# A linear attention stage with its tiles turned: tokens on partitions for x, z, B and y, features on partitions for C and the logits

## The reference, cut to what matters

```python
proj = x @ W_in.T                      # xp 512, z 512, B 256, C 256, dt_low 16
dt = softplus(dt_low @ dt_W.T + dt_b)
dAcs = cumsum(dt * A, axis=2)          # within a chunk
scores = einsum('bcihn,bcjhn->bcijh', Cc, Bc) * Lm * dtc[:, :, None, :, :]
y_intra = einsum('bcijh,bcjhp->bcihp', scores, xc)
chunk_state = einsum('bckhn,bckhp->bchnp', Bc, wx)
y_cross = einsum('bcthn,bchnp,bcth->bcthp', Cc, h_states, exp(dAcs))
y = y_intra + y_cross + xp * D_param
y = y / sqrt(mean(y * y) + 1e-6) * norm_w * silu(z)
return y @ W_out.T
```

## Time and profile before

| what | value |
|---|---|
| median of 3 runs | 3202.09 us (3197.8 to 3204.78) |
| profiled execution, own time | 3200.55 us |
| its span, first to last instruction | 3198.5 us |
| PE busy | 3052.5 us, 95% |
| DVE busy | 2336.9 us, 73% |
| ACT busy | 1671.4 us, 52% |
| POOL busy | 1176.2 us, 37% |
| chain that ended last | PE 91%, DVE 5% |
| largest line in it | PE L769, 48% |

### The profile page before, as it was taken

The page is one execution under the profiler, slowest core; times in us unless marked ns, Lnnn a source line. Parts: engine busy times, 40 slices in busy tenths (PEclk is TensorE's granted clock), DMA queues, the critical chain, the costliest instruction groups (busy, mean ns, idle before and its releaser), DMA issues.

```text
span 3198.5 us, 121249 instructions
## 1 busy us (share of the span) xinstructions
PE 3052.5 (95%) x52488; PEld 2729.7 (85%) x52488; DVE 2336.9 (73%) x4256; ACT 1671.4 (52%) x3803; POOL 1176.2 (37%) x2287
## 2 busy tenths in 40 slices
PE   7999999999999999999999999998777777999999
PEld 6999999999999999999999999997666666888887
DVE  6887887887887887887887887887444445777775
ACT  5555555555555555555555555554333332555555
POOL 3554554554554554554554554553000001000000
PEclk9999999999999999999999999999999997999999
DMA  3211111111111111111111111112544344768765
GB/s 116 73 52 52 46 50 53 47 53 50 46 54 50 46 54 50 46 54 50 46 54 50 47 53 50 48 46 81 200 115 119 106 129 130 224 212 236 222 207 159
DMA packets 336353, 285.87 MB, mean 89 GB/s; under 512 B 52160, under 2 KB 265792, under 8 KB 334928
## 3 DMA queue, kind: packets, MB, share of 16 engines
q1 hardware_dynamic: 335248, 277.95, 29.3%
q10 hardware_dynamic: 576, 0.17, 0.0%
HBM read 164.80 MB, written 113.25 MB: 87 GB/s over the span
## 4 chain that ended last, share of the span: by engine, by line
PE 91%; DVE 5%; issue 3%; DMA 1%; ACT 0%; SPq 0%; POOL 0%; DVEq 0%; POOLq 0%; ACTq 0%
PE a_bank L769 48%; PE s_rt L1422 8%; PE g_pick_ps L1182 5%; PE s_w_ps L1408 5%; PE a_bank L828 4%; PE s_sum L1435 4%; PE a_bank L861 4%; DVE g_picked L1151 3%; PE g_acc_ps L1203 2%; PE a_bank L777 2%; PE a_bank L846 2%; PE a_bank L796 2%; PE a_bank L786 1%; PE a_bank L788 1%; PE a_bank L928 1%
## 5 line engine op out<-in xcount | busy, mean ns | idle before, releaser
L769 PE MATMUL a_bank<-xnTh,wdh 128*128 128x256 f32 x2048 | 591.1, 289 | 1.4 <-DVE permT L692 1.4
L769 PE MATMUL a_bank<-xnTl,wdh 128*128 128x256 f32 x2048 | 578.9, 283 | 0.0
L769 PE MATMUL a_bank<-xnTh,wdl 128*128 128x256 f32 x2048 | 578.8, 283 | 0.0
L359 POOL TENSOR_TENSOR ve<-mv,ln_eps 128x1 f32<-128x1 f32 x128 | 78.5, 613 | 918.0 <-DVE mv L604 918.0
L1372 ACT COPY s_res<-s_rt 128x512 f32<-128x512 f32 x512 | 263.1, 600 | 291.2 <-PE s_rt L1422 291.2
L1378 DVE TENSOR_TENSOR s_resT<-s_w_ps,s_b 128x2048 f32<-128x2048 f32 x128 | 293.3, 2291 | 155.8 <-PE s_w_ps L1408 155.8
L769 PEld LDWEIGHTS a_bank<-xnTh,wdh 128*128 128x128 f32 x2048 | 391.6, 191 | 9.6 <-issue 1.6
L769 PEld LDWEIGHTS a_bank<-xnTl,wdh 128*128 128x128 f32 x2048 | 391.8, 191 | 2.9
L769 PEld LDWEIGHTS a_bank<-xnTh,wdl 128*128 128x128 f32 x2048 | 391.8, 191 | 0.0
L635 DVE COPY_PREDICATED scan_in<-mask,a_bank 64x512 f32<-64x512 uint32 x512 | 378.7, 740 | 16.8 <-PE a_bank L828 4.7
L668 DVE TENSOR_SCALAR xs<-gs,mg 64x128 f32<-64x128 f32 x960 | 300.9, 375 | 56.1 <-PE a_bank L861 49.0
(11 more groups left out here) (126 smaller groups left out, 6913.1 us busy)
## 6 DMA issues: line engine op xcount, KB each, us to landing
x<-in_x_dram SPq DMA_DIRECT2D x128, 256.0 KB, 3.2
xn_dram<-xn SPq DMA_DIRECT2D x128, 256.0 KB, 2.2
part_dram<-res SPq DMA_DIRECT2D x128, 256.0 KB, 2.4
g_xn<-xn_dram SPq DMA_DIRECT2D x128, 256.0 KB, 3.0
s_w<-in_w_dram SPq DMA_DIRECT2D x128, 256.0 KB, 3.9
s_part<-part_dram SPq DMA_DIRECT2D x128, 256.0 KB, 3.8
out_dram<-s_out SPq DMA_DIRECT2D x128, 256.0 KB, 2.9
g_w<-in_w_dram SPq DMA_DIRECT2D x4, 2048.0 KB, 12.4
```

The source lines that it names most:

```text
L769: last = nc.tensor.matmul(out, lhs[a], rhs[c], start=(k == 0 and n == 0), stop=(k == nk - 1 and n == 2))
```

## The change

The attention phase is laid out anew:

- x and z are projected with tokens stationary and 512 columns moving (`project_x`, `project_z`), B and dt as before (272 columns). C and the logits are projected with their weights stationary and 256 tokens moving (`project_c`, `project_logits`), so C, the logits and x need no transposes.
- `scores` uses tiles of 32 rows: two heads each, `cexp` has 2 heads in place of 4, and the four row groups write to four banks.
- `scan` has `scan_in` stationary (64 columns, a chunk's tokens) and `xs` moving (32 columns), two column halves in turn; y comes out with tokens on partitions.
- C is not scaled by the decay any more; y is, after the scan (`scale_y` on DVE). POOL multiplies x by D (`skip_x`) and adds it (`add_skip`); the sum of squares comes from ACT's accumulator, and `sum_squares` and its POOL sums go.
- `norm_w` is folded into `W_out`, and y times SiLU(z) is transposed on PE (`transpose_yz`) before the output projection.
- The bias and tie breaker of the logits move from POOL to DVE, in `picks`.
- The four banks of the scan hold scores in one half, states or y in the other; one bank (`mix`) serves the transposes of `xn`, those of y and the output.
- The order on each engine is new. In the first step `project_x` waits for the weights of x and z.

The core of the diff:

```diff
+        def skip_x(n):
+
+            pool.wait_ge(x_cp, n + 1)
+            wait(pool, yv_cp, n)
+            for c in range(2):
+                rows_ = token_rows(c)
+                nc.gpsimd.tensor_tensor(dx[rows_, :], xs[c][n % 4][rows_, :, :].rearrange("t h d -> t (h d)"), d_row[rows_, :],
+                                        ALU.mult).then_inc(dx_cp, 1)
+                pool.wait_ge(dx_cp, 2 * n + c + 1)
+
+        def add_skip(n):
+            pool.wait_ge(yt_cp, n + 1)
+            wait(pool, sq_cp, n)
+            wait(pool, yz_cp, n)
+            nc.gpsimd.tensor_tensor(yv[:], yt[:], dx[:], ALU.add).then_inc(yv_cp, 1)
...
+        def scale_y(n):
+
+            dve.wait_ge(y_ps, 2 * n + 2)
+            wait(dve, yv_cp, n)
+            gain = e1[:, n // 2 % 2, n % 2, :].rearrange("p (b h) -> p b h", b=2).unsqueeze(3).to_broadcast([P, 2, H // 2, HD])
+            nc.vector.tensor_tensor(yt[:].rearrange("p (b h d) -> p b h d", b=2, h=H // 2),
+                                    scan_bank[:, 2:4, HALF:512].rearrange("p b (h d) -> p b h d", h=H // 2), gain,
+                                    ALU.mult).then_inc(yt_cp, 1)
+
+        def gate(n):
+            dve.wait_ge(yv_cp, n + 1)
+            dve.wait_ge(z_cp, n + 1)
+            wait(dve, yzT_ps, n - 1)
+            nc.vector.tensor_tensor(yz[:, n % 2, :], yv[:], sz[:, n % 4, :], ALU.mult).then_inc(yz_cp, 1)
+
...
+        def picks(s):
+
+            dve.wait_ge(lg_ps, s + 1)
+            wait(dve, pm, 3 * s)
+            groups = ST // GRP
+            view = lg[:].rearrange("p (g t) -> p g t", t=GRP)
+            nc.vector.scalar_tensor_tensor(view, proj[1][:, 0:ST].rearrange("p (g t) -> p g t", t=GRP), bc_col[:],
+                                           tie_row[:].unsqueeze(1).to_broadcast([P, groups, GRP]), ALU.add, ALU.add).then_inc(pm, 1)
+            dve.wait_ge(pm, 3 * s + 1)
+            nc.vector.tensor_reduce(gmax[:], view, AX_X, ALU.max).then_inc(pm, 1)
+            dve.wait_ge(pm, 3 * s + 2)
+            wait(dve, pm_out[s % 2], 16 * (s // 2))
+            nc.vector.tensor_tensor(permT[:, s % 2, :].rearrange("p (g t) -> p g t", t=GRP), view,
+                                    gmax[:].unsqueeze(2).to_broadcast([P, groups, GRP]), ALU.is_equal).then_inc(pm, 1)
+
+        for q in range(NG):
+            nc.vector.memset(state_view(0, 0)[:, q, :, :], 0.0).then_inc(g_ready, 1)
...
-        def project_tokens(n, b, i, read, count):
-
-            for half, (c0, c1) in enumerate(((0, C_C), (C_C, TCOLS))):
-                wait(pe, read, count - 1 + half)
-                for k in range(KD):
-                    last = split_mm(bank[PROJ0 + half][:, 0:c1 - c0], [t[:, k, i * P:(i + 1) * P] for t in xnT[b]],
-                                    [w[:, k, c0:c1] for w in wt], k, KD)
-                last.then_inc(tok_ps, 1)
-
-        def project_features(b, j):
-
-            for m in range(2):
-                f = (2 * j + m) * P
-                for k in range(KD):
-                    last = split_mm(bank[PROJ0 + j % 2][:, m * ST:(m + 1) * ST], [w[:, k, f:f + P] for w in wd],
-                                    [t[:, k, :] for t in xnT[b]], k, KD)
-            last.then_inc(d_ps, 1)
-
...
+        def project(out, n, weights):
+
+            for k in range(KD):
+                last = split_mm(out, [t[:, k, :] for t in tile_of(n)], [w[:, k, :] for w in weights], k, KD)
+            return last
+
+        def project_bdt(n):
+            if n % 2 == 0:
+                wait(pe, z_cp, n)
+            else:
+                wait(pe, pm, 3 * (n // 2) - 2)
+            project(proj[n % 2][:, 0:C_C], n, [w[:, :, 0:C_C] for w in wt]).then_inc(bdt_ps, 1)
+
+        def project_x(n):
+            if n == 0:
+                pe.wait_ge(w_lo, LAST_STAGE)
+            if n % 2 == 0:
+                pe.wait_ge(bdt_cp, n + 1)
+            else:
+                pe.wait_ge(x_cp, n)
+            project(proj[0][:], n, [w[:, :, 0:DI] for w in wd]).then_inc(x_ps, 1)
+
+        def project_z(n):
+            if n % 2 == 0:
+                pe.wait_ge(bdt_cp, n + 2)
+            else:
+                pe.wait_ge(x_cp, n + 1)
+            project(proj[1 - n % 2][:], n, [w[:, :, DI:2 * DI] for w in wd]).then_inc(z_ps, 1)
+
+        def project_features(s, out, cols):
+
+            for m, c0 in enumerate(cols):
+                for k in range(KD):
+                    last = split_mm(out[:, m * ST:(m + 1) * ST], [w[:, k, c0:c0 + P] for w in wt], [t[:, k, :] for t in xnT[s % 2]], k, KD)
+            return last
+
+        def project_c(s):
+            pe.wait_ge(z_cp, 2 * s + 1)
+            project_features(s, proj[1], (C_C, C_C + P)).then_inc(c_ps, 1)
+
+        def project_logits(s):
+            pe.wait_ge(c_cp, s + 1)
+            project_features(s, proj[1], (C_L,)).then_inc(lg_ps, 1)
+
...
+        def transpose_yz(n, mixed):
+            pe.wait_ge(yz_cp, n + 1)
+            pe.wait_ge(xnT_lo, mixed)
+            wait(pe, res_cp, n)
+            for k in range(KI):
+                last = nc.tensor.transpose(mix[:, k * P:(k + 1) * P], yz[:, n % 2, k * P:(k + 1) * P], ident[:])
+            last.then_inc(yzT_ps, 1)
...
-        def scores(n):
-            wait(pe, bt_cp, n + 1)
-            wait(pe, cexp_cp, n + 1)
-            for f in range(2):
-                for c in range(2):
-                    for w in range(2):
-                        own = c_rows(w)
-                        last = nc.tensor.matmul(bank[SC0 + w][c * CH:(c + 1) * CH, f * 4 * CH:(f + 1) * 4 * CH],
-                                                BCT[own, f, c * CH:(c + 1) * CH], cexp[own, f, c, :, :], start=True, stop=True)
-                        if f == 1 and c == 1:
-                            last.then_inc(sc_ps, 1)
-
...
+        def scores(n):
+            pe.wait_ge(bT_cp, n + 1)
+            pe.wait_ge(cexp_cp, n + 1)
+            for f in range(2):
+                for c in range(2):
+                    for r in range(4):
+                        own = slice(32 * r, 32 * r + 32)
+                        last = nc.tensor.matmul(scan_bank[c * CH:(c + 1) * CH, r, f * P:(f + 1) * P],
+                                                BT[own, f, c * CH:(c + 1) * CH], cexp[own, f, c, :, :], start=True, stop=True)
+                        if f == 1 and c == 1:
+                            last.then_inc(sc_ps, 1)
+
...
         def scan(n):
-            wait(pe, mt_cp, 4 * n + 4)
-            wait(pe, yv_cp, 4 * n)
-            for c in range(2):
-                wait(pe, cs_cp[c], n + 1)
-                wait(pe, g_ready, 8 * n + 8 + 4 * c)
-                for h in range(H):
-                    rows_ = slice(32 * (h % 4), 32 * (h % 4) + 32)
-                    col = (h // 4) * P + c * CH
-                    last = nc.tensor.matmul(bank[YB][rows_, col:col + CH], xs[c][:, h, :], scan_in[c][:, h, :], start=True, stop=True)
-                last.then_inc(scan0 if c == 0 else y_ps, 1)
-
+            pe.wait_ge(mt_cp, 4 * n + 4)
+            pe.wait_ge(cs_cp[0], n + 1)
+            pe.wait_ge(cs_cp[1], 2 * n + 2)
+            pe.wait_ge(g_ready, states_ready(n, 1))
+            for h in range(H):
+                for c in range(2):
+                    last = nc.tensor.matmul(scan_bank[token_rows(c), 2 + h // 8, HALF + h % 8 * HD:HALF + (h % 8 + 1) * HD],
+                                            scan_in[c][:, h, :], xs[c][n % 4][:, h, :], start=True, stop=True)
+                    if h == H - 1:
+                        last.then_inc(y_ps, 1)
...
+        for s in range(NST + 2):
+            n0, n1, n2 = 2 * s, 2 * (s - 1), 2 * (s - 2)
+            if valid(s):
+                wait(pe, xnT_lo, n0 + 2)
+                project_bdt(n0)
+            if valid(s + 1):
+                transpose_xn(n0 + 2, 0)
+            if valid(s):
+                project_bdt(n0 + 1)
+            if valid(s - 1):
+                transpose_b(n1)
+            if valid(s):
+                project_x(n0)
+            if valid(s - 2):
+                transpose_yz(n2, min(n0 + 3, NT))
+            if valid(s - 1):
+                chunk_states(n1)
+                scores(n1)
+            if valid(s):
+                project_z(n0)
+            if valid(s - 1):
+                transpose_b(n1 + 1)
+            if valid(s - 2):
+                project_out(n2)
+            if valid(s):
+                sums(s)
+            if valid(s - 1):
+                scan(n1)
+
+            if valid(s + 1):
+                transpose_xn(n0 + 3, 1)
+            if valid(s):
+                spread_gains(s)
+                project_x(n0 + 1)
+            if s == NST + 1:
+                pe.wait_ge(z_cp, NT)
+                pe.wait_ge(pm, 3 * NST)
+                gather["transpose_picks"](pe, 0)
+            if valid(s - 2):
+                transpose_yz(n2 + 1, min(n0 + 4, NT))
+            if valid(s - 1):
+                chunk_states(n1 + 1)
+                scores(n1 + 1)
+            if valid(s):
```

(63 more changed lines are left out.)

838 lines of the change are left out of this document (357 added, 481 removed).

## The result

The changed kernel takes 3265.57 us (median of 4 runs, 3263.9 to 3273.16), the kernel before 3202.26 beside it: a ratio of 1.0204, with an interval of 1.0184 to 1.0223. It is slower by 63.3 us. The prediction was 3190 us, between 3100 and 3262, so both the direction and the range were wrong. The profiled execution took 3265.26 us (span 3263.5).

A forecast was written before the change was run, and what follows sets the result against it. PE was taken to bound the attention phase (busy 479.77 of 480 us). Its terms, -2.24 us without the scan and +2.04 with it, gave -0.20 a step, x 63 = -13 us, +1 for the ends: 3190 us, range 3100 to 3262.

The forecast's parts named there:

- projections' intervals: PE's projections: 229 ns between 512-column matmuls, 36 matmuls fewer, 24.24 to 23.81 us a step, -0.43.
- Scores' 32 records: PE's `scores`: eight array tiles at work, about 0.69 us in place of 1.09, -0.80 us a step.
- loads free: Rival at `scan`: weight loads cost nothing, scan stays at 1.10 us or lower, -141 us, 3062; 12%.
- in series: Rival at each `scan`: loads and moves in series, 80 ns a round, 2.67 us, +57 us, 3259; 15%.
- not eight at a time: Rival at `scores`: 32-row tiles do not run eight at a time, scores stay 1.09 us, 3240; 5%.
- the scan's term: PE's `scan` with 64 columns loaded, 32 moved: 62 ns a round, 2.12 us, +2.04 us a step.
- The net of all PE terms: PE's whole step: -2.24 us without the scan, +2.04 with it, -0.20 a step.
- The other engines lie beside PE, and I cost them at nothing: DVE, ACT, POOL and SP work costs nothing; two close handovers have 1 and 1.5 us to spare.
- the cover for `dA`: POOL's chain before `sums`: 8 to 8.5 us within the 10 us behind the copy of dt, 1.5 to spare.
- the mask's cover: DVE before the first tile's `scan`: y's low part, states piece and mask need 5.2 of 6.2 us, 1 to spare.
- a new wait: Rival: mask or POOL's chain to `dA` late, PE waits every step, 6.3 us per 0.1 us, 3253 at 1 us; 18%.
- the ends: First step's `project_x` waiting for weights and the draining steps: +1 us, between -3 and +5.

The follow-up runs named there:

- b1: Kernel before with only the scan's operands swapped (64 columns loaded, 32 moved); output layout not what the rest expects: 3318.53 us, ratio 1.0371.
- x12: Changed kernel with x loaded before the marks' store on SP and the first `skip_x` behind `step_sizes` (`dA`) on POOL: 3194.2 us, ratio 0.9984.
- x1: Changed kernel with only SP's order altered, the load of x ahead of the marks' store: 3256.63 us, ratio 1.0178.
- x3: Changed kernel with each scan matmul split in two of 32 loaded columns, so four column groups take turns: 3298.51 us, ratio 1.0316.
- x4: Changed kernel with both moves of x12 and the scan split over four column groups: 3171.45 us, ratio 0.9911.
- x6: x4 with DVE's low part of `xn` ahead of the statistics of the next x in the second half step: 3135.58 us, ratio 0.9791.
- x7: x6 with each scan cut into two halves of heads, other work between: 3156.88 us, ratio 0.986.

## Why the prediction was wrong

**PE's prices held.** The projections' intervals are the old ones (229 ns at 512 columns). Scores' 32 records span 0.69 us in the order of time, as forecast (0.62 in the chain), which four array tiles at a time would not have given; transposes behind a scan 0.59, elsewhere 0.44. For the scan 2.12 us and a round of 62 ns were forecast; its 64 records span 2.06, less the 0.22 of a last record and over 31 rounds 59 ns. Two readings behind these forecasts don't come out: L938's seven rounds in 0.264 us are 38 ns each and not 36, and the terms given for scores (three rounds of 105 to 129 ns and a last record of 0.271) add up to 0.59 to 0.66, so 0.69 was met with some luck. The weight loads are what the round was worked out from (kernel after, by form, 1000 to 1400 us; line, count, then busy us and mean ns):

```profile
L930 PEld LDWEIGHTS a_scan<-xs,scan_in 128*64 128x64 f32 x1434 | 43.9, 138 | 2.0 <-issue 0.2
...
L896 PEld LDWEIGHTS a_scan<-xs,raw 64*32 64x32 f32 x736 | 11.3, 106 | 3.9 <-issue 3.9
```

The rivals *loads free* (scan 1.1 us) and *in series* (2.67) fell with that, and so did *not eight at a time* (scores 1.09). b1 gives the scan's term alone: +120.7 us against 63 x 2.04 = 129, the difference being the 59 for 62 ns. The net of all PE terms was -0.20 us a step; x12, where PE alone sets the pace, has 33.93 for 34.11, -0.18.

The Trainium skill's rule that the prediction set against the row ("TensorE: Matmul & The Clock Gate", Part 3, "The mechanism": loads overlap only where the row group differs) would have given 80 ns a round. The trace disagrees: 59 ns, with every record on all 128 rows. What the runs show instead is a dependence on column groups: two of them with 64 loaded columns give 2.06 us, four with 32 give 1.29, though twice as many records run.

**The step that failed is "The other engines lie beside PE, and I cost them at nothing"**, and in it two sentences. The first is "SP issues the same transfers. The store of the marks moves behind `picks` at the step's end". It is true and stops short. The store now waits for the last thing in the step, and nothing was asked of what stands behind it in SP's queue: the part's store and the load of x. Nor did the cover for `dA`, "8 to 8.5 us, with 1.5 to spare", start from that load. POOL's chain from the variance to `dA` took 9.16 us (1006.58 to 1015.74), 0.7 to 1.2 more than that, which alone would have fitted. But it was counted from the copy of dt, whose second tile ACT has ready at 1004.90, and it started at 1006.58, when the statistics of the late x were there: 1.7 us later. From 1004.90 to 1014.87 10.0 us were to be had; 1.68 + 9.16 = 10.84 were used, with 0.04 for the handover, and PE lost 0.91.

The second is the mask's cover, "so 5.2: 1 us to spare". The states' pieces were priced at the 1.30 us of the earlier trace rows, a row beside which POOL did nothing long. The change itself puts `skip_x` on POOL, and where the two meet they take 3.3 to 3.8. In the kernel after this cost nothing, since the late load also delayed `skip_x`, and the pieces ahead of the mask took 1.18. With the load in time (x1) they meet: 2 us more where 1 was to spare, and a step 0.95 us longer than x12's. So the cover for `dA` is what failed in the measured time, and the mask's would have failed in its place.

**The sum over.** A gain of 12 us was forecast, and x12, without the waits, has 5.7 (3194.2 for 3199.86). Of the difference, 1 us is less gain over the phase, and the ends cost 4 to 5 us for the forecast 1 (the tail behind the last `mg` is 1008.3 before, 1013.6 in x12); the rest is within the spread of the runs. What x12's two moves take away puts 71.4 us on top, 3265.6; by the mean step it is (35.03 - 33.93) x 63 = 69, and 3 us are in the tail.

**The rival that came true** is "a new wait", given 18%. Its price, 6.3 us for each 0.1 us in a step, was right: 1.10 us a step is 69 us. It had been forecast with POOL's long pieces as the cause; they are one half of it, and what made them late, SP's order, was not in it. It was priced out only to 1 us a step (3253), and the range, whose upper end was set beside the series case, ended 3.6 us short.

## What to carry to other kernels

When a change moves an instruction that waits, write down for every in-order queue what stands behind it, and follow the first load there to its last reader: here a store of marks held up a load, and the price appeared 14 us later on PE. A cover of 1 us in a step of 34 is no cover until every piece in it has been priced beside what the other engine will be doing at that time. And a swap of matmul operands must be priced by what is loaded as well as by what is moved: the same scan cost nearly twice as much with 64 columns loaded and 32 moved as the other way round, which used up nearly all that the rest of the change had gained.

## What the runs showed of the hardware that was not expected

- DVE's `tensor_scalar` from SBUF to SBUF in float32 is held up while POOL multiplies tensors: 1.11 to 1.18 us for four pieces alone, 3.30 and 3.78 beside 2.65 us of POOL. `COPY_PREDICATED`, which reads PSUM, is not: four take 3.06 us beside POOL and 3.02 without.
- Two matmuls of 32 loaded columns are cheaper than one of 64: 128 records in 1.29 us, 64 in 2.06.
- In kernels with the split scan PE stops for 1 to 3 us inside groups of small matmuls, with no semaphore that it waits for, and all 80 of them over 0.4 us in x3, x4, x6 and x7 (200 to 2150 us) end 2.2 to 2.9 us behind the start of a packet of the instruction queue. PE's idle time between 400 and 1900 us is 111.5 us in x3 (the wait for `dA` among it), 24.2 in x6 and 4.8 in x12, which has no split.
- Behind such stops the granted clock could fall to its lower level: in x3 nine times, for 41 us in 1950, with 512-column matmuls 427 ns apart in place of 229. In the kernels before and after it never fell in these 1950 us.
